# Where the transposes stand in the loop, and how wide the projection matmuls are, in a fused attention layer

## The reference

```python
q = (x @ Wq.T).reshape(b, n, 12, 32)
k = (x @ Wk.T).reshape(b, n, 12, 32)
v = (x @ Wv.T + bv).reshape(b, n, 12, 32)
scores = jnp.einsum('bqhd,bkhd->bhqk', q, k) * 384 ** -0.5 + (adj + adj)[:, None]
row_nonzero = jnp.any(scores != 0, axis=-1, keepdims=True)
scores = jnp.where(row_nonzero, scores, -jnp.inf)
p = jnp.nan_to_num(jax.nn.softmax(scores, axis=-1))
out = jnp.einsum('bhqk,bkhd->bqhd', p, v).reshape(b, n, 384) @ Wo.T + bo
result = layernorm(x + out)
```

## Time and profile before

| | |
|---|---|
| median of 3 runs | 620.27 us (620.02 to 621.94) |
| the profiled execution | 619.91 us |
| its span, first to last instruction | 617.7 us |
| granted clock of TensorE, mean | 0.998 |
| TensorE, ScalarE, VectorE, GpSimd busy | 98%, 81%, 77%, 66% |
| chain that ended last | TensorE 91%, VectorE 4% |
| transfers | 58.5 MB, 95 GB/s over the span |

### The profile page before, as it was taken

One profiled execution on the slowest core, in us unless ns is written; L12 is line 12 of the kernel. 1 busy time (PEld: TensorE's weight loads), 2 busy tenths in 40 slices (PEclk: granted clock), 3 DMA queues, 4 the chain that ended last, 5 costly groups with the idle time before them and its releaser, 6 DMA issues.

```text
span 617.7 us, 22924 instructions
## 1 busy us (share of the span) xinstructions
PE 606.6 (98%) x8250; PEld 503.2 (81%) x8250; DVE 477.6 (77%) x2376; ACT 503.3 (81%) x1944; POOL 410.5 (66%) x499
## 2 busy tenths in 40 slices
PE   9999999999999999999999999999999999999996
PEld 5788888888888888888888888888888888888774
DVE  4677877877877877877877877877877877877886
ACT  4788878879788788878879788788878879778893
POOL 0676767767667676767767667676767767656663
PEclk9999999999999999999999999999999999999999
DMA  9410423222242321434222242421423221222111
GB/s 300 152 38 22 135 90 129 86 75 88 83 141 83 125 84 37 134 90 129 87 79 85 82 140 79 136 81 36 131 89 129 87 78 37 79 89 84 54 53 52
DMA packets 33424, 58.51 MB, mean 95 GB/s; under 512 B 9888, under 2 KB 22688, under 8 KB 33312
## 3 DMA queue, kind: packets, MB, share of 16 engines
q1 hardware_dynamic: 32880, 56.47, 28.6%
q10 hardware_dynamic: 432, 0.59, 0.3%
HBM read 43.52 MB, written 13.53 MB: 92 GB/s over the span
## 4 chain that ended last, share of the span: by engine, by line
PE 91%; DVE 4%; issue 1%; POOLq 0%; ACT 0%; DVEq 0%; POOL 0%
PE qk_ps L343 34%; PE vo_ps L375 15%; PE vo_ps L431 15%; PE scores_ps L360 9%; PE scores_ps L388 8%; PE att_ps L411 8%; DVE nscores L577 2%; PE qk_ps L431 2%; DVE stats L661 1%; DVE y L658 1%; DVE att_t L649 0%; DVE att_ps L607 0%; PE qk_ps L329 0%; DVE recip L613 0%; DVE probs_t L592 0%
## 5 line engine op out<-in xcount | busy, mean ns | idle before, releaser
L483 ACT ACTIVATE probs<-nscores,neg_max 128x128 f32<-128x128 f32 x768 | 298.1, 394 | 85.2 <-DVE neg_max L577 85.2
L577 DVE CUSTOM_DVE_ANT_0 nscores<-scores_ps,adj_n 128x128 f32<-128x128 f32 x768 | 167.3, 287 | 23.6 <-PE scores_ps L360 22.3
L292 POOL TENSOR_TENSOR tree<-nscores 128x768 f32<-128x768 f32 x64 | 120.2, 1878 | 59.4 <-DVE neg_max L577 58.0
L483 ACT ACTIVATION_READ_ACCUMULATOR probs<-nscores,neg_max 128x1 f32 x768 | 147.4, 192 | 0.0
L375 PE MATMUL vo_ps<-w_v,x_t 128*128 128x384 f32 x576 | 111.8, 338 | 0.0
L274 POOL TENSOR_TENSOR x_t<-x_raw,x_t 128x512 fp32r<-128x512 f32 x45 | 59.0, 1314 | 79.2 <-ACT x_t L500 79.2
L292 POOL TENSOR_TENSOR tree<-tree 128x384 f32<-128x384 f32 (+1 forms) x128 | 103.9, 812 | 10.0
L343 PE MATMUL qk_ps<-x_t,w_q 128*128 128x512 f32 x405 | 110.6, 411 | 0.0
L343 PE MATMUL qk_ps<-x_t,w_k 128*128 128x512 f32 x405 | 110.4, 411 | 0.0
L375 PEld LDWEIGHTS vo_ps<-w_v,x_t 128*128 128x128 f32 x576 | 102.4, 188 | 6.0
L431 PE MATMUL vo_ps<-w_o,att_t 128*128 128x384 f32 x522 | 101.6, 339 | 0.0
(11 more groups left out here) (71 smaller groups left out, 681.3 us busy)
## 6 DMA issues: line engine op xcount, KB each, us to landing
x_n<-xn SPq DMA_DIRECT2D x32, 384.0 KB, 5.4
out<-out_n SPq DMA_DIRECT2D x31, 384.0 KB, 5.0
x_raw<-xt SPq DMA_DIRECT2D x15, 768.0 KB, 6.5
scale_t<-scale_mem SPq DMA_DIRECT2D x58, 192.0 KB
adj_n<-adj SPq DMA_DIRECT2D x32, 128.0 KB, 4.5
scale_mem<-scale_rows SPq DMA_DIRECT2D x58, 16.0 KB
x_raw<-xt SPq DMA_DIRECT2D x3, 256.0 KB, 5.3
nscores<-wq ACTq DMA_DIRECT2D x3, 192.0 KB, 4.0
```

Of the source, the lines that this page charges most:

```text
L292: nc.gpsimd.tensor_tensor(tree[:, b % 2, :, 0:width], src[:, :, 0:width], src[:, :, width:2 * width], ALU.add).then_inc(tree_step, 1)
L483: last = nc.scalar.activation(probs[:, b % 2, h], nscores[:, b % 2, h], ACT.Exp, bias=neg_max[:, b % 2, h:h + 1], scale=-1.0, accum_out=ro ...
L577: last = nc.vector.tensor_tensor_reduce(out=nscores[:, half, h], in0=scores_ps[j][:, m * P:(m + 1) * P], in1=adj_n[:, b // 2 % 2, half], s ...
```

## The change

Order. TensorE's slot becomes `turn(b)`, `score(b+1)`, a whole tile of projection, `values(b+1)`, half a tile, `project_out(b-1)`, `attend(b)`. VectorE's begins with `normalise(b-1)` and `find_scale(b)`, then two thirds of the bias steps, `attention_low`, the last third, the high copy, `keep_first`, `keep_v`, and ends with `residual(b-1)`. ScalarE's begins with `attention_high(b-1)` and the copies of the transposes (three of four now, `LOWS`), then all twelve heads, then `keep_second`.

Banks. The transposes go to `qk_ps[0]`, `v_ps`, `qk_ps[1]` and a spare bank (`turn_ps`). The attention product goes to `scores_ps[1]` and the output to `scores_ps[0]`. So `score` waits for `att_done` and `y_ready`, `project` and `values` for the copies of the transposes, `turn` for the keeps, `project_out` and `attend` for the bias steps. The scaled attention goes to `att_n` in SBUF, the sums of `find_scale` to SBUF as well.

Projection. Each slot has nine matmuls of 512 columns and nine of 256 (the first or second half of the third tile of each pair of slots). GpSimd's tree sums heads 0 to 7 and 8 to 11 apart. Only the last example is `direct`, and the products of zeros go, but for the three at the start.

```diff
--- before.py
+++ after.py
...
 REST = P >> TREE
+
+PARTS = ((0, 2 * HPT), (2 * HPT, HEADS))
+STEPS = TREE * len(PARTS)
 XBUFS = 3
+
...
 
...
@@ -89,12 +96,15 @@
 
         scores_ps = [ps(f"scores_ps{j}", [P, 512]) for j in range(HPT)]
         qk_ps = [ps(f"qk_ps{i}", [P, 512]) for i in range(2)]
-        vo_ps = ps("vo_ps", [P, 512])
-        att_ps = ps("att_ps", [P, 512])
+        v_ps = ps("v_ps", [P, 512])
+        spare_ps = ps("spare_ps", [P, 512])
+
+        turn_ps = [qk_ps[0], v_ps, qk_ps[1], spare_ps]
+        att_ps = scores_ps[1]
 
 
         scale_mem = nc.dram_tensor("scale_mem", (2, D, P), F32, kind="Internal").ap()
-        first_ps = [*scores_ps, qk_ps[1], vo_ps]
...
@@ -157,46 +168,29 @@
             if value > 0:
...
         def direct(b):
 
-            return ending(b + 1)
...
+            return b == NB - 1
...
         def out_bank(b):
-            return qk_ps[b % 2] if ending(b + 1) else vo_ps
...
+            return scores_ps[0] if has(b + 1) else scores_ps[2]
...
         def projected(b):
 
 
-            if b < -1 or ending(b):
-                return (), ()
+            if not -1 <= b < NB - GRP - 1:
+                return ()
             tile = (b + 1) // 2 * 3
             if b % 2 == 1:
-                return ((tile, 0, FULL),), ((tile + 1, 0, PART),)
-            return ((tile + 1, PART, FULL), (tile + 2, 0, PART)), ((tile + 2, PART, FULL),)
+                return (tile, 0, GRP * P), (tile + 1, 0, GRP * P // 2)
+            return (tile + 2, 0, GRP * P), (tile + 1, GRP * P // 2, GRP * P)
+
+        def slots_with_tiles(b):
+
+            return min(b + 2, NB - GRP)
...
         def turned_bank(b, j):
-            return scores_ps[j][:, 0:columns(b) * D].rearrange("p (h q) -> p h q", q=D)
+            return turn_ps[j][:, 0:columns(b) * D].rearrange("p (h q) -> p h q", q=D)
...
             def sum_scores(b):
 
-                pool.wait_ge(biased, KT * (b + 1))
                 wait(pool, total_done, b - 1)
-                src = nscores[:, b % 2]
-                for n in range(TREE):
-                    width = P >> (n + 1)
-                    if n:
-                        pool.wait_ge(tree_step, b * TREE + n)
-                    nc.gpsimd.tensor_tensor(tree[:, b % 2, :, 0:width], src[:, :, 0:width],
-                                            src[:, :, width:2 * width], ALU.add).then_inc(tree_step, 1)
-                    src = tree[:, b % 2]
+                for part, (low, high) in enumerate(PARTS):
+                    pool.wait_ge(biased, KT * b + high // HPT)
+                    src = nscores[:, b % 2, low:high]
+                    for n in range(TREE):
+                        width = P >> (n + 1)
+                        if n:
+                            pool.wait_ge(tree_step, b * STEPS + part * TREE + n)
+                        nc.gpsimd.tensor_tensor(tree[:, b % 2, low:high, 0:width], src[:, :, 0:width],
+                                                src[:, :, width:2 * width], ALU.add).then_inc(tree_step, 1)
+                        src = tree[:, b % 2, low:high]
...
-            def project(tile, first, end):
+            def project(b, n, tile, start, end):
 
                 g, t = tile // TILES + 1, tile % TILES
                 w, cols = (w_k, w_q)[t // KT], slice(t % KT * P, (t % KT + 1) * P)
-                if first == 0:
-                    wait(pe, kept, tile - 1)
-                    if tile == 1:
-                        pe.wait_ge(first_keys, KT)
-                for i in range(first, end):
-                    k, (a, c) = i // len(TERMS), TERMS[i % len(TERMS)]
-                    if t == 0 and i % len(TERMS) == 0:
+
+                if b >= 0:
+                    pe.wait_ge(turned_low, LOWS * b + (1, 3)[n])
+                elif n:
+                    pe.wait_ge(first_keys, KT)
+                for k in range(KT):
+                    if t == 0:
                         pe.wait_ge(x_split, KT * (g - 1) + k + 1)
-                    last = nc.tensor.matmul(qk_ps[tile % 2][:], w[:, a, k, cols], x_t[:, g % XBUFS, c, k],
-                                            start=(i == 0), stop=(i == FULL - 1))
-                if end == FULL:
-                    last.then_inc(proj_done, 1)
+                    for i, (a, c) in enumerate(TERMS):
+                        last = nc.tensor.matmul(qk_ps[n][:, start:end], w[:, a, k, cols], x_t[:, g % XBUFS, c, k, start:end],
+                                                start=(k == 0 and i == 0),
+                                                stop=(k == KT - 1 and i == len(TERMS) - 1))
+                last.then_inc(proj_done, 1)
 
             def score(b):
...
                 elif b % GRP == 0:
-                    pe.wait_ge(kept, TILES * g)
+                    pe.wait_ge(kept_first, slots_with_tiles(b - 2))
+                    pe.wait_ge(kept_second, slots_with_tiles(b - 2))
+
                 wait(pe, biased, KT * b)
+                wait(pe, y_ready, b - 2)
+                wait(pe, att_done, b - 1)
...
+                if b > 0:
+                    pe.wait_ge(turned_low, LOWS * (b - 1) + 2)
...
+                        last = nc.tensor.matmul(v_ps[:, 0:HID], x_t[:, g % XBUFS, a, k, cols], w_v[:, c, k],
...
             def turn(b):
 
-                pe.wait_ge(biased, KT * (min(b + 1, NB - 1) + 1))
...
+                pe.wait_ge(kept_first, slots_with_tiles(b - 1))
+                pe.wait_ge(kept_second, slots_with_tiles(b - 1))
+                pe.wait_ge(v_ready, b + 1)
...
-                        last = nc.tensor.transpose(scores_ps[j][:, h * D:(h + 1) * D], probs[rows, b % 2, h],
+                        last = nc.tensor.transpose(turn_ps[j][:, h * D:(h + 1) * D], probs[rows, b % 2, h],
                                                    ident[rows, rows])
...
             def attend(b):
-                pe.wait_ge(turned_low, low_copies(b))
-                pe.wait_ge(turned_high, high_copies(b))
+                pe.wait_ge(turned_low, LOWS * (b + 1))
+                pe.wait_ge(turned_high, b + 1)
                 pe.wait_ge(v_ready, b + 1)
-                if has(b + 1):
-                    wait(pe, att_split, b)
+                free_scores(b + 1)
+                if not has(b + 1):
+                    pe.wait_ge(att_done, b)
...
+            def free_scores(b):
+
+                pe.wait_ge(biased, KT * min(b + 1, NB))
...
             def project_out(b):
                 pe.wait_ge(att_split, b + 1)
...
-                free_out_bank(b)
+                free_scores(b + 2)
+                wait(pe, y_ready, b)
...
             for b in range(-1, NB + 1):
-                ahead, behind = projected(b)
+                if has(b):
+                    turn(b)
                 if has(b + 1):
                     score(b + 1)
-                for tile, first, end in ahead:
-                    project(tile, first, end)
-                if has(b + 1):
+                for n, (tile, start, end) in enumerate(projected(b)):
+                    project(b, n, tile, start, end)
+                    if n == 0:
+                        values(b + 1)
+                if has(b + 1) and not projected(b):
                     values(b + 1)
-                if ending(b) and has(b):
-                    free_out_bank(b - 1)
-                    run_idle(1, out_bank(b - 1))
+                if has(b - 1):
+                    project_out(b - 1)
                 if has(b):
-                    turn(b)
-                for tile, first, end in behind:
-                    project(tile, first, end)
-                if b == NB - 1:
-                    run_idle(1, out_bank(b - 1))
                     attend(b)
-                    project_out(b - 1)
-                else:
-                    if has(b - 1):
-                        project_out(b - 1)
-                    if has(b):
-                        attend(b)
 
         @block.scalar
         def _(act):
...
-                if t == 0:
-                    wait(act, scores_done, (g - 1) * GRP)
+                act.wait_ge(proj_done, 2 * b + 4)
+
+                wait(act, scores_done, (g - 1) * GRP)
                 dst, scale = ((k_t, 1.0), (q_t, 0.5 * SCALE))[t // KT]
-                nc.scalar.activation(dst[:, g % 2, t % KT], qk_ps[tile % 2][:], ACT.Copy, scale=scale).then_inc(kept, 1)
+                nc.scalar.activation(dst[:, g % 2, t % KT, start:end], qk_ps[1][:, start:end], ACT.Copy,
+                                     scale=scale).then_inc(kept_second, 1)
 
...
                     nc.scalar.activation(turned_rows(b, j), turned_bank(b, j), ACT.Copy).then_inc(turned_low, 1)
 
...
                 act.wait_ge(att_done, b + 1)
                 wait(act, oproj_done, b - 1)
...
 
...
             for b in range(-1, NB + 2):
-                ahead, behind = projected(b)
-                if has(b - 1) and direct(b - 1):
+                if has(b - 1):
                     attention_high(b - 1)
-                if has(b + 1):
```

(72 more changed lines are left out.)

76 lines of the change are left out of this document (28 added, 48 removed).

## The result

The changed kernel takes **638.19 us** (median of 4 runs, 637.14 to 639.33), 1.0287 times the kernel before (620.14 us in four runs; 95% interval 1.0259 to 1.0314): it is slower. Its profiled execution has a span of 635.4 us at a mean granted clock of 0.993.

What follows compares the result with a forecast made beforehand. TensorE's own work bounds the kernel before; the change adds a VectorE wait. Slots 10.3, memory 3.6, start 1, end 0 make +15 on a 617.7 span, plus 2.2: 635 us, range 628 to 642.

Steps and rivals of the forecast that it cites:

- A: Start of attend(b-1) on TensorE, from which the prediction counts the times in a slot, in us.
- 57 slots: Slot 2 to slot 58, where the chain is whole: 0.18 us more each, 10.3 in all.
- memory, in these slots: The scale's round trip through memory, late in the 12 slots after an x_raw load: 0.3 us each, 0 to 1.0.
- start: First transposes wait for example 0's twelve exponentials and a keep: 1 us more, between 0 and 2.
- end: Four slots without projection, 7.8 us each as the output projection waits for the last bias: net 0, within 2.
- The wait that the change adds: Scores wait for normalise, queued behind the residual on VectorE: TensorE idles 0.44 us a slot, 25 us in all.
- TensorE follows VectorE: Delay from normalise's end on VectorE to the scores' start on TensorE: 0.05 us.
- The wait for the copy: Before the projection, TensorE waits for ScalarE's first copy of the transposes to free qk_ps[0]: 0.06 us more lost.
- The half tile: Nine 256-column projection matmuls a slot: 0.117 us each, 1.05 in all.
- the rival in which the load binds: Each 256-column matmul costs 0.188 us, slot +0.64, 57 of them 36 us: about 671; chance 0.10.
- The shape changes: Moving the transposes beside the scores removes two TensorE tile-shape changes a slot; values fall from 1.68 to 1.57; 0.32 gained.
- gives back a little: Dropping the products of zeros at the end gains slightly, about offset by the last output projection's wait for the residual.

Runs made afterwards that it cites:

- the 128-column run: Changed kernel with each half tile of 9 matmuls of 256 columns made as two of 9 with 128 columns, twice the weight loads; 692.9 us.
- two other runs: Changed kernel with VectorE's queue reordered to add, scaling, statistics: 633.8 us; and that kernel with find_scale between scaling and statistics: 647.8 us.

## Why the prediction was right, point by point

| step | predicted | measured |
|---|---|---|
| scaling ends | A+1.96 | A+1.93 |
| scores start | A+2.01 | A+2.07 |
| projection starts | A+2.95 | A+2.95 |
| values; half tile | 1.57; 1.05 | 1.58; 1.06 |
| slot | 9.44 | 9.465 |
| 57 slots | +10.3 | +11.7 |
| memory, in these slots | +3.6 | 0 |
| start | +1 | +2.05 |
| end | 0 | +3.9 |
| span | +15 | +17.7 |

The last column is of the profiled executions, and its parts add up to 17.7 within rounding.

- **The wait that the change adds** is the cause, in place and size: add, statistics, aggregate, scaling without a gap, 0.35 us of idle in each slot ahead of the scores. The run with the statistics twice shows it from one side. From the other side the undisturbed slots of 9.00 show it, with the statistics behind the scaling. The idle was forecast at 0.44 and 25 us in all; it is 0.35 and 22.6.
- **TensorE follows VectorE** by 0.14 here (302.22 to 302.36), and not by the 0.05 that I took from the earlier trace rows. The wait for the copy that I had put at 0.06 isn't there, so the errors cancel at the projection.
- **The half tile** has 0.117 a matmul, and the rival in which the load binds is ruled out, by a hair that the 128-column run measures.
- **The shape changes** give what they were priced at: values 1.58 against 1.68 before.
- **Memory was over-sized.** I took the load of x_raw to keep the second transfer back to A+7.5, by its distance from the load's issue. It was issued between A+5.1 and A+6.2 behind such loads (A+5.04 in ordinary slots), which is 2.0 to 3.1 behind the rows, where the earlier trace rows has 3.08: it goes by the rows, and these now leave earlier. No scaling in the 57 slots waited for the memory by the profile, where I had said 12. One slot is longer by 0.37, with 0.27 of idle on VectorE for which the profile names no releaser. What I had right in kind, that the trip is nearly bare, shows once the time left for it falls from 7.8 to 6.6.
- **Start and end were under-sized**, each in part by the clock. At the start 1.33 of the 2.05 are nine matmuls in 3.54 and not 2.2. At the end 1.37 of the 3.9 are the last output projection, which takes 3.22 where it was 1.85. Its row in TensorE's timeline, and the busy times of two stretches in it:

```profile
626.55 3.22 PE L430 MATMUL scores_ps<-w_o,att_t 128*128 128x384 f32 x9 [2.39 <-DVE y L639]
```

```profile
627.00:628.00 1.00, 1.00 (x5) 1.00 (x5) 0.19 (x2) 0.00 (x0) 0.61 (x2) 0.50 0.00 0
628.00:629.00 1.00, 1.00 (x5) 1.00 (x4) 0.00 (x0) 0.46 (x1) 0.40 (x2) 0.50 0.00 0
```

  The change took the products of zeros away, and I had priced that as "gives back a little". They stood in gaps, and the clock in the kernel before stayed at 1.00 over them. The four slots without projection are 8.03, 8.47, 8.08 and 8.69, 2.1 in all above my 7.8 each; but before they weren't 7.8 either, and against the kernel before (32.6 in all) they are only 0.7 longer. The last slot is 1.0 longer, and what follows the last attend 2.2, the 1.37 in it. In the four, the values wait 0.27 for a copy that the projection used to hide, and in two of the slots the scaling was late.

The forecast of 635 is 3.2 us below the measured 638.19. Its main term, the slots, is right by its mechanism. That the sum comes out as near as this is in part luck: memory was 3.6 too large, start and end together 4.9 too small.

## What to carry to other kernels

When a result moves into a bank that the next stage overwrites, write out what stands ahead of the freeing instruction in its engine's queue: that chain, and not the engine's load, is the new length of the loop. When you then take the chain away, ask what each remaining input of the freed instruction costs if it is wanted that much earlier; here undisturbed slots went from 9.46 to 9.00, but a trip through memory held the mean at 9.30, and with that gone it was 9.13, with a late `find_scale`. Read the first and last slots by themselves: they took back what the loop had gained. Moving a small operand from PSUM to SBUF can tie a two-input VectorE instruction to what GpSimd does beside it, as the traces here show; no run moved the operands back.

## What the runs showed of the hardware

- A VectorE instruction with two SBUF inputs and 12 columns lasted up to 1.32 us beside a GpSimd instruction, 0.17 without. With one of the two in PSUM, 121 executions beside GpSimd lasted at most 0.18.
- Eighteen pairs of a 128x128 weight load and a 128-column matmul followed each other in 0.109 us, though a load's record is 190 ns long.
- TensorE idle for 1.39 us at the start and 2.39 us at the end was followed by stretches at 1.2 GHz, a granted 0.50. The same idle at the start of two other runs (1.40 and 1.37) was not. The 0.35 us of idle in each slot left the clock at 1.00. With products of zeros in the gap it was 1.00 behind it.
- A 512-column product of fp32 zeros takes 0.87 us; nine matmuls of that width on rounded data take 2.2.
- 192 KB read back from memory into all partitions came 4.8 to 5.7 us after the issue in the 32 slots that waited for it with 512 or 768 KB of loads issued behind it, and within 4.7 with none.
